# Products of queries and keys as four column tiles, and new sequences of steps, in a fused RWKV-7 and gated-FFN layer

## The chip, the cores and the metric

One NeuronCore of a Trainium2 chip. The metric is the device time of one call in microseconds. All tensors are float32.

## The reference

The input is normalised over its 256 channels; a recurrent attention block (RWKV-7 with 4 heads of 64) and a gated FFN both read the normalised input, and their product is added to the input. Cut to what matters:

```python
# x: (2, 4096, 256)
xn = layernorm(x)
# attention: token-shift mixes, projections to r, w, k, v, kk, a, g, then per head
S = S * d_t + (S a_t) b_t^T + v_t k_t^T       # a_t = -kk, b_t = kk * a, d_t = exp(w_t)
y_t = S r_t
s = (groupnorm(y) * ln_w + ln_b + (r.k.faaaa).v) * g @ w_output.T
# FFN with integer weights / 127
f = silu((silu(xn @ wg.T) * (xn @ wu.T)) @ wd.T)
out = x + s * f
```

The recurrence is computed in chunks of 32 steps. Within a chunk each step's query reads the keys of the earlier steps (for `a`) or of the earlier steps and its own (for `r`), so a matrix of 32 keys by 32 steps is wanted for each of two kinds of query (`a`, `r`), two kinds of key (`k`, `b`), each head and each batch; a mask keeps the part below the diagonal.

## The kernel before

**Tiling.** The 4096 steps are cut into 16 blocks of 256 steps of both batches (512 columns, 8 chunks of 32 steps for each batch; `NT` = 16, `L` = 32). Channels lie on the partitions in two halves (`NH` = 2, two heads each).

**Sections.** The outer loop runs over sections. In section i, block i+1 is normalised and mixed (`norm`, letter L), block i goes through projections and keys (`mixing` F, `decays` D, `key` K, `receptance` R, `value` V, `update` E, `pairs` X), block i-1 through the FFN (`ffn` N) and the recurrence (`back` B), block i-2 through the output (`output` O). On each engine every stage is a generator that yields after each step; the order of the steps is written out by hand as a string of letters for each engine (`ORDER`, with `FIRST` and `LAST` for the sections at the ends), and `walk` takes one step of the named stage for each letter. So each engine's instruction order is fixed, and the engines meet only at semaphores.

**PSUM.** Four banks form a ring (`ring`, `room` waits until a bank's last content was taken); four more (`chunk_banks`) belong to the recurrence and, early in a section, to the projections.

**Pairs.** `pairs` goes through a block in four quarters `qt` (one half of the channels, that is two heads on the 128 partitions, by 4 of the 8 chunks, `n`, with the batch `b` inside). VectorE makes the keys of a quarter in `KSb`: for each group `j` of 8 steps, 64 columns, 32 for the keys `k` and 32 for the keys `b`, each scaled for that group (steps `near`, `far`, `keys`). ScalarE makes the queries in `qpad`, 32 columns for each chunk and group: two heads (each with zeros on the other head's partitions) by two kinds of query by 8 steps. On TensorE the steps `half` and `matrix` multiply them (line 509): weights are the 64 keys of one chunk and group, 128 partitions, the 32 columns of queries stream, and the result goes to 64 partitions of the bank, partitions 0 to 63 for batch 0 and 64 to 127 for batch 1. All 64 keys are multiplied for each group `j`, also those that lie behind the group's steps; VectorE's `copy_predicated` (line 1156) takes from the bank only what the mask lets through. The step `KT` transposes the keys for the state (line 517). The ring's bank for quarter `qt` is free again when VectorE's copy is done (`am_ready`).

**Back.** For each of 8 chunks `c` the recurrence goes TensorE (`state`, line 614), ScalarE (`rhs`, line 904), TensorE (`u`, line 628), VectorE and ScalarE (lines 1206, 910), TensorE (`s`, line 642), VectorE (state, line 1211), with GpSimd's fading of the state (line 1325) beside it; the outputs `values` (589) and `y` (598) fill in.

Names used below: `gate..`, `up..`, `down..` are the FFN's products (lines 534 and 544), `k0`, `k1`, `hk`, `gh`, `v..` projections (line 380), `out0`, `out1` the output's products (line 664).

Of the kernel before, what the change touches and what calls it, by code (L numbers as in the profile page):

```python
# [21 lines left out]
L = 32  # L22
BL = 8
# [24 lines left out]
for _n, _w in (("ident", 128), ("bd", 128), ("center", 128), ("am0", 256), ("ti", HL * HL)):  # L48
# [1 line left out]
    _at += _w  # L50
CTOT = _at

ORDER = {"pe": ("NNNFNKOOFNNORVNNNNKKOVKRBNKBNRNNVBBNBBNBNBNBBVNNBBEBVBBNBBVBNBBNBBXBXBBNXBBNBNBBXBBXBXBBNBBLBNBBXXBB"
            "LXXXXLL"),
         "act": ("NFKFFFFFRFVNKKNVOKKKBEBOKRKRDXXBXBVNBVNBBVVNBBBXBVVBBXBBBBNBBXXBLBBLXLBXBBNBBLXX"),
         "dve": ("ONBOOBBBBBDBBBBBBBNBBDBBDDOOKKDXEFKKNDEDEXDKEEBXBXXXNBXBXXXBEXXBEXXBXNBXLBXXXBXXBLXBXNXXXBXXXBXLXLBX"
             "XXBBXXLLLLLLLL"),
         "pool": ("DBBBBBBLBBLBLLLLLLLL")}
FIRST = {"pe": ("NFKFKKNNNNNVNNKVRKRVNRVVNNNNNNNNNNNNNNNNNVEXXXNXXXLXXXXXLXLLN"),
         "act": ("NNKFFFNFNNFFKFKVKKKEVKKRRXXDRVVVVVVXXXNNXNLXXLLXXLX"),  # L60
         "dve": ("DNDDDNFKKEDNKKDXEXDDENKEXXXLEXXXXXXLXXXEXEXXXXXXXXNXXXXXXXXXXXLLXXLLLLLLLNL"),
         "pool": ("DLLLLLLLLLL")}
LAST = {"pe": ("NOOONONNNNNNNNNBBNNNBBBBBNBBBBBNBBBBBNBBBBBNBBBNBBNBBBBBNBBBBBNBBBNBBNNNNN"),
        "act": ("NONNOBBNBBBBBBBBNBBBBBBBBBNBBBBBBBBNN"),
        "dve": ("BOOOBBBBBBBBBBBBBBBBONONNBBBBBBBBBBBNBBBBBNBN"),
        "pool": ("BBBBBBBBB")}
NB = 4

class Signal:
# [51 lines left out]
def program(nc, d):  # L121
    with ExitStack() as ctx:
# [128 lines left out]
        pe, act, dve, pool, sp = nc.tensor, nc.scalar, nc.vector, nc.gpsimd, nc.sync  # L251
# [86 lines left out]
        def sections():  # L338
            for i in range(-1, NT + 2):
                yield tuple(t if 0 <= t < NT else None for t in (i + 1, i, i - 1, i - 2))  # L340

        def run(engine, norm, mixing, decays, key, receptance, value, update, pairs, ffn, back, output, convert):
            for tn, tf, tb, to in sections():
                streams, order = {}, LAST if tn is None and tf is None else FIRST if tb is None and to is None else ORDER
                if tn is not None:
# [13 lines left out]
        def pe_program():  # L359

            def room(key, emptied):

                o, before = ring.take(key, emptied)
                if before:
                    pe.wait_ge(*before)
                return o
# [132 lines left out]
            def pairs(t):  # L499
                for qt in range(NK):  # L500
                    K, Q, E = KSb[qt % 2], qpad[qt % 2], KE[qt % 2]
                    o = room((t, "A", qt), am_ready(t, qt + 1))
                    pe.wait_ge(*q_made(t, qt + 1))
                    pe.wait_ge(*keys_made(t, qt + 1))
                    for n in range(QC // 2):
                        for j in range(NJ):
                            for b in range(B):
                                oc = o[64 * b:64 * b + 64, 128 * n:128 * n + 128].rearrange("p (x e) -> p x e", e=L)
                                q = pe.matmul(oc[:, :, BL * j:BL * j + BL], K[:, 2 * n + b, 64 * j:64 * j + 64],  # L509
                                              Q[:, 2 * n + b, j, :, :, :].rearrange("p a b e -> p (a b) e"), start=True, stop=True)  # L510
                        if n == 1:
                            yield f"half{qt}"
                    q.then_inc(*ring.fill((t, "A", qt)))
                    yield f"matrix{qt}"
                    o = room((t, "KT", qt), kt_ready(t, qt + 1))
                    for n in range(QC // 2):
                        q = pe.transpose(o[:, 128 * n:128 * n + 128], E[:, 2 * n:2 * n + 2, :].rearrange("p q n -> p (q n)"), ident)  # L517
                    q.then_inc(*ring.fill((t, "KT", qt)))
                    yield f"KT{qt}"
# [150 lines left out]
            pe.wait_ge(s_set, NSET)  # L670
            pe.wait_ge(s_clear, NCLEAR)
            run("pe", norm, mixing, decays, key, receptance, value, update, pairs, ffn, back, output, convert)


# [841 lines left out]
```

## Time and profile before

| | us |
|---|---|
| median of 3 runs | 1608.94 (1607.33 to 1612.72) |
| span of the profiled execution | 1603.4 |
| around the span, median less span | 5.5 |
| TensorE matmul busy | 1520.5 (95%) |
| VectorE busy | 1243.6 (78%) |
| ScalarE busy | 1069.5 (67%) |
| GpSimd busy | 354.6 (22%) |

The profile counts an engine as busy from an instruction's start to its end; TensorE's matmuls overlap one another, so their busy time is the time in which at least one runs. PE stands for TensorE's matmuls, PEld for its weight loads, DVE for VectorE, ACT for ScalarE, POOL for GpSimd. "A<-B, C" names the tile written and those read, "128*64" the rows and columns of the array, "128x32" the partitions and columns that stream. The chain that ended last is followed back from the last instruction to whatever released each one.

### The profile page before, as it was taken

The page shows a single profiled execution, that of the slowest core. Times are in us where ns is not written, and L with a number is a line of the kernel's source. Part 1 is how long each engine was busy: PE and PEld are TensorE (multiplying, and loading weights), DVE is VectorE, ACT ScalarE, POOL GpSimd, SP SyncE. Part 2 cuts the span into 40 slices and gives each one's busy share as a digit, 9 for nine tenths or more (in the row PEclk, how much of TensorE's full clock was granted, in tenths as well). Part 3 has the DMA queues.
Part 4 walks back from the last instruction along what each step waited for, and adds up shares of the span by engine and source line. Part 5 has one row for each costly group of instructions (what it writes and reads, how often), then busy time and mean ns, then how long its engine had stood idle before and what let it go on. Part 6 is the DMA issues. An engine that isn't in the chain of part 4 may idle for free.

```text
span 1603.4 us, 48245 instructions
## 1 busy us (share of the span) xinstructions
PE 1520.5 (95%) x20288; PEld 1064.9 (66%) x20288; DVE 1243.6 (78%) x2661; ACT 1069.5 (67%) x1889; POOL 354.6 (22%) x362
## 2 busy tenths in 40 slices
PE   3699999999999999999999999999999999999887
PEld 1366767576676757667676676757667675766765
DVE  2968787787878878887887878778787887888643
ACT  3758586685857758685775858668585775768512
POOL 3121402313040131302213140231304013130201
PEclk9799999999999999999999999999999999999999
DMA  4011110301212021111202111030121202111020
GB/s 149 14 25 29 33 34 16 62 18 32 43 25 47 16 55 25 33 34 24 56 16 39 42 34 34 16 62 19 33 42 25 48 16 55 25 33 34 12 56 28
DMA packets 251430, 57.85 MB, mean 36 GB/s; under 512 B 223696, under 2 KB 250704, under 8 KB 251088
## 3 DMA queue, kind: packets, MB, share of 16 engines
q1 hardware_dynamic: 241936, 41.95, 13.9%
q10 hardware_dynamic: 9280, 12.81, 2.2%
q8 instruction: 162, 2.65, 0.7%
q14 instruction: 52, 0.43, 0.1%
HBM read 36.38 MB, written 18.35 MB: 34 GB/s over the span
## 4 chain that ended last, share of the span: by engine, by line
PE 92%; DVE 3%; ACT 2%; issue 1%; POOL 0%; DMA 0%; SPq 0%; ACTq 0%; DVEq 0%; POOLq 0%
PE bank L534 23%; PE chunk L380 15%; PE bank L544 11%; PE bank L509 8%; PE bank L664 4%; PE chunk L642 3%; PE chunk L614 3%; PE chunk L589 3%; PE chunk L598 2%; PE bank L485 2%; PE bank L380 2%; PE bank L517 2%; PE bank L479 2%; PE chunk L628 2%; DVE VU L981 1%
## 5 line engine op out<-in xcount | busy, mean ns | idle before, releaser
L1325 POOL TENSOR_TENSOR SF<-ST,CT 128x256 f32<-128x256 f32 x128 | 99.7, 779 | 728.8 <-DVE ST L1211 728.8
L534 PE MATMUL bank<-xT,wg 128*128 128x256 f32 x768 | 197.2, 391 | 14.2 <-DVE VU L981 13.5
L534 PE MATMUL bank<-xT,wu 128*128 128x256 f32 x768 | 207.3, 395 | 0.0
L544 PE MATMUL bank<-wd,hT 128*128 128x256 f32 x768 | 176.8, 383 | 1.9 <-DVE hT L1171 1.9
L534 PEld LDWEIGHTS bank<-xT,wg 128*128 128x128 f32 x768 | 136.3, 189 | 57.6 <-DVE VU L981 24.1
L544 PEld LDWEIGHTS bank<-wd,hT 128*128 128x128 f32 x768 | 143.3, 190 | 29.3 <-issue 7.2
L534 PEld LDWEIGHTS bank<-xT,wu 128*128 128x128 f32 x768 | 135.1, 188 | 34.8 <-issue 14.5
L380 PE MATMUL chunk<-KS,W 128*128 128x512 f32 x320 | 149.6, 598 | 0.3 <-ACT gT L719 0.3
L509 PE MATMUL bank<-qpad,KS 128*64 128x32 f32 x4096 | 141.2, 226 | 4.0 <-DVE KE L1143 4.0
L887 ACT ACTIVATE Y<-chunk 32x256 f32<-32x256 f32 x256 | 96.3, 376 | 70.9 <-PE chunk L598 67.0
L509 PEld LDWEIGHTS bank<-qpad,KS 128*64 128x64 f32 x4096 | 130.7, 141 | 14.1 <-issue 9.0
L380 PE MATMUL chunk<-big,W 128*112 128x512 f32 (+1 forms) x256 | 117.9, 593 | 5.1 <-POOL big L1284 2.9
L861 ACT ACTIVATE sg<-bank 128x512 f32<-128x512 f32 x96 | 57.1, 595 | 86.4 <-PE bank L534 84.5
L1171 DVE TENSOR_TENSOR hT<-sg,bank 128x512 f32<-128x512 f32 x96 | 65.7, 684 | 53.0 <-ACT sg L861 35.2
L904 ACT ACTIVATE rhs<-chunk 96x256 f32<-96x256 f32 x128 | 48.5, 379 | 87.3 <-PE chunk L614 86.3
L1206 DVE COPY VU<-chunk 32x256 f32<-32x256 f32 x128 | 53.4, 417 | 63.3 <-PE chunk L628 62.1
L380 PEld LDWEIGHTS chunk<-KS,W 128*128 128x128 f32 x320 | 59.2, 189 | 62.9 <-issue 48.5
L830 ACT ACTIVATE qpad<-big 64x256 f32<-64x256 f32 x256 | 92.2, 407 | 1.9
L1284 POOL TENSOR_TENSOR KS<-VU,xT 128x512 f32<-128x512 f32 x64 | 89.0, 1424 | 0.0
L1284 POOL TENSOR_TENSOR big<-VU,xT 128x512 f32<-128x512 f32 x64 | 74.4, 1198 | 48.4 <-DVE VU L981 48.4
L1211 DVE TENSOR_TENSOR ST<-SF,chunk 128x256 f32<-128x256 f32 x128 | 53.8, 420 | 37.2 <-PE chunk L642 34.4
L380 PEld LDWEIGHTS chunk<-big,W 128*112 128x112 f32 (+1 forms) x256 | 46.5, 182 | 49.7 <-issue 39.4
(156 smaller groups left out, 3231.3 us busy)
## 6 DMA issues: line engine op xcount, KB each, us to landing
smalls<-in_x SPq DMA_DIRECT2D x32, 256.0 KB, 3.1
Y<-in_x SPq DMA_DIRECT2D x32, 256.0 KB, 3.0
out<-fsil ACTq DMA_DIRECT2D x32, 256.0 KB, 2.6
scrA<-AM SPq DMA_DIRECT2D x64, 64.0 KB, 1.9
hat<-scrB SPq DMA_DIRECT2D x32, 128.0 KB, 3.1
hat<-scrF SPq DMA_DIRECT2D x32, 128.0 KB, 3.1
KE<-scrA SPq DMA_DIRECT2D x64, 32.0 KB, 2.2
scrT<-KE SPq DMA_DIRECT2D x16, 128.0 KB, 1.7
```

Source lines behind the costliest of these rows:

```text
L380: m = pe.matmul(o, weights[:, h, :], x[:, h, :], start=(h == 0), stop=(h == NH - 1))
L509: q = pe.matmul(oc[:, :, BL * j:BL * j + BL], K[:, 2 * n + b, 64 * j:64 * j + 64], Q[:, 2 * n + b, j, :, :, :].rearrange("p a b e -> p (a ...
L534: q = pe.matmul(o[:, TT_ * n2:TT_ * n2 + TT_], w[:, h, 128 * (n + n2):128 * (n + n2) + 128], x_now[:, h], start=(h == 0), stop=(h == NH - 1))
L544: q = pe.matmul(o[:, 256 * m:256 * m + 256], hT[:, n, 128 * m:128 * m + 128], wd[:, n, :], start=(n == 0), stop=(n == NF - 1))
L664: q = pe.matmul(o[:, 256 * n2:256 * n2 + 256], yb[:, h, 128 * m:128 * m + 128], wo[:, h, :], start=(h == 0), stop=(h == NH - 1))
L830: i = act.activation(Q[p0:p0 + 64, :, :, hh, x, :], own[p0:p0 + 64, qs], ACT.Copy)
L861: act.activation(sg[:, :], ring.tile(key)[:, :], ACT.Silu).then_inc(*sg_ready.up)
L887: i = act.activation(by_batch, RY[64 * x + 32:64 * x + 64, :, :].rearrange("p b (g n) -> p b g n", g=NH), ACT.Copy)
L1171: i = dve.tensor_tensor(hT[:, n:n + 2, :], sg[:, :].rearrange("p (n c) -> p n c", n=2), ring.tile(key)[:, :].rearrange("p (n c) -> p n c", ...
L1211: dve.tensor_tensor(ST[:, :, :, :].rearrange("p b h n -> p b (h n)"), SF[:, :, :, :].rearrange("p b h n -> p b (h n)"), PS, ALU.add).then_ ...
L1284: pool.tensor_tensor(columns(dst[:, h, :]), columns(w[:, h, :]), x_now_of(par, h), ALU.add).then_inc(*moved.up)
L1325: pool.tensor_tensor(SF[:, :, :, :], ST[:, :, :, :], fade[:, c].unsqueeze(3).to_broadcast([128, B, NH, N]), ALU.mult).then_inc(*faded.up)
```

## The change

In `pairs` on TensorE the product of one chunk and group `j` is cut in two calls, one for each kind of key `x`. Each takes only the keys up to the end of the group, `BL * j + BL` = 8, 16, 24 or 32 columns of weights, and writes as many partitions from partition `64 * b + 32 * x` on. So four column tiles of up to 32 columns are used in turn (batch 0 `k`, batch 0 `b`, batch 1 `k`, batch 1 `b`) where two of 64 were used. The streamed queries are the same 32 columns. The strings of steps are new for all sections and all engines but GpSimd's in `FIRST` and `LAST`.

```diff
-ORDER = {"pe": ("NNNFNKOOFNNORVNNNNKKOVKRBNKBNRNNVBBNBBNBNBNBBVNNBBEBVBBNBBVBNBBNBBXBXBBNXBBNBNBBXBBXBXBBNBBLBNBBXXBB"
-            "LXXXXLL"),
-         "act": ("NFKFFFFFRFVNKKNVOKKKBEBOKRKRDXXBXBVNBVNBBVVNBBBXBVVBBXBBBBNBBXXBLBBLXLBXBBNBBLXX"),
-         "dve": ("ONBOOBBBBBDBBBBBBBNBBDBBDDOOKKDXEFKKNDEDEXDKEEBXBXXXNBXBXXXBEXXBEXXBXNBXLBXXXBXXBLXBXNXXXBXXXBXLXLBX"
-             "XXBBXXLLLLLLLL"),
-         "pool": ("DBBBBBBLBBLBLLLLLLLL")}
+ORDER = {"pe": ("NNNFNKOONFNOKKVONNNNRKRVBKBNNRNNBBNBBNVBNBNBBVNBBEBNVBBVBBNBNBBNBBXBXBBXNBBNBXBBNBBXBXBBNBBLBXXBBNBB"
+                "XLXXXLL"),
+         "act": ("NFKFFFFNFFKKNOVORKKKVBEBKKRRXDXBXBNVNBVBBVVBNBBVVXBBBXBBBXNXBBBBLBBXLLBXBBNBBXLX"),
+         "dve": ("OBNOBBOBBBBDBBBBBDBOBBBNBDODKKEXDKKFDNEXEDDKEEBXBXXXNBXBXXEXEBXBXXXXBXXBLNBXXBXXXBXXBXLNXXXXBXXBXLXB"
+                "LXBXBXLLLLLLLL"),
+         "pool": ("BDBBBBLBLBBBLLLLLLLL")}
...
                     for n in range(QC // 2):
                         for j in range(NJ):
                             for b in range(B):
-                                oc = o[64 * b:64 * b + 64, 128 * n:128 * n + 128].rearrange("p (x e) -> p x e", e=L)
-                                q = pe.matmul(oc[:, :, BL * j:BL * j + BL], K[:, 2 * n + b, 64 * j:64 * j + 64],
-                                              Q[:, 2 * n + b, j, :, :, :].rearrange("p a b e -> p (a b) e"), start=True, stop=True)
+                                for x in range(2):
+                                    p0, keys = 64 * b + L * x, BL * j + BL
+                                    oc = o[p0:p0 + keys, 128 * n:128 * n + 128].rearrange("p (x e) -> p x e", e=L)
+                                    q = pe.matmul(oc[:, :, BL * j:BL * j + BL], K[:, 2 * n + b, 64 * j + L * x:64 * j + L * x + keys],
+                                                  Q[:, 2 * n + b, j, :, :, :].rearrange("p a b e -> p (a b) e"), start=True, stop=True)
                         if n == 1:
                             yield f"half{qt}"
                     q.then_inc(*ring.fill((t, "A", qt)))
```

## Rows read from the trace of the kernel before

**Rows 1.** The page: busy us, share of the span, instructions.

```profile
PE 1520.5 (95%) x20288; PEld 1064.9 (66%) x20288; DVE 1243.6 (78%) x2661; ACT 1069.5 (67%) x1889; POOL 354.6 (22%) x362
```

**Rows 2.** The page: chain that ended last, by engine and by line.

```profile
PE 92%; DVE 3%; ACT 2%; issue 1%; POOL 0%; DMA 0%; SPq 0%; ACTq 0%; DVEq 0%; POOLq 0%
PE bank L534 23%; PE chunk L380 15%; PE bank L544 11%; PE bank L509 8%; PE bank L664 4%; PE chunk L642 3%; PE chunk L614 3%; PE chunk L589 3%; PE chunk L598 2%; PE bank L485 2%; PE bank L380 2%; PE bank L517 2%; PE bank L479 2%; PE chunk L628 2%; DVE VU L981 1%
```

**Rows 3.** Busy time by engine in two sections; columns in the first line.

```profile
core 0: us, PE busy (x) PEld busy (x) DVE busy (x) ACT busy (x) POOL busy (x), PEclk, DMA share, GB/s
759.50:854.70 95.20, 93.81 (x1269) 65.89 (x1269) 77.64 (x167) 66.61 (x118) 22.16 (x23) 1.00 0.17 34
664.40:759.50 95.10, 93.43 (x1267) 65.42 (x1265) 76.89 (x166) 66.66 (x118) 21.39 (x22) 1.00 0.16 34
```

**Rows 4.** Waits of PE from 759.5 to 854.7: us, times, longest.

```profile
PE bank L534 <- DVE VU L981: 1.8, 2, 0.9
PE chunk L420 <- issue: 0.4, 1, 0.4
```

**Rows 5.** Busy time of line 509 alone in that section: PE, then PEld.

```profile
759.50:854.70 95.20, 8.62 (x256) 7.95 (x256) 1.00 0.17 34
```

**Rows 6.** The chain in order of time: start us, us, what.

```profile
823.42 1.06 PE bank L509 x32
...
844.14 1.99 PE bank L509 x64
846.12 0.39 PE chunk L642 x16
846.52 0.39 PE chunk L598 x16
846.91 1.91 PE bank L380 x4
```

**Rows 7.** Timeline of PE: start us, us to the last end, instructions merged.

```profile
844.07 2.06 PE L509 MATMUL bank<-qpad,KS 128*64 128x32 f32 x64
846.05 0.46 PE L642 MATMUL chunk<-VU,KT 64*64 64x64 f32 x16
```

**Rows 8.** The chain, at a section's start: streams of 512, 256 and 128 columns.

```profile
762.40 1.72 PE chunk L380 x4
764.11 0.86 PE bank L534 x4
...
766.69 0.87 PE bank L655 x8
```

**Rows 9.** Timeline of PE: weights 64 wide, 64 and 16 columns.

```profile
790.61 1.15 PE L563 MATMUL bank<-hat 64*64 64x64 f32 x32
...
793.70 1.06 PE L571 MATMUL bank<-KE,hat 64*64 64x16 f32 x32
```

**Rows 10.** Timeline of PE: first and last start of two groups of eight.

```profile
843.62 0.28 PE L598 MATMUL chunk<-VU,AM 32*64 32x64 f32 x4
...
843.78 0.22 PE L628 MATMUL chunk<-rhs,TT 32*64 32x64 f32 x1
...
843.81 0.22 PE L598 MATMUL chunk<-VU,AM 32*64 32x64 f32 x1
843.84 0.22 PE L628 MATMUL chunk<-rhs,TT 32*64 32x64 f32 x1
...
843.87 0.22 PE L598 MATMUL chunk<-VU,AM 32*64 32x64 f32 x1
```

**Rows 11.** Section 0: its window (columns of rows 3), then the chain.

```profile
70.70:90.00 19.30, 16.30 (x277) 15.29 (x278) 18.67 (x52) 8.21 (x19) 0.00 (x0) 0.61 0.01 2
...
73.70 3.63 PE bank L509 x64
...
78.37 3.56 PE bank L509 x64
...
84.69 2.56 PE bank L509 x64
...
87.84 1.99 PE bank L509 x64
```

**Rows 12.** Busy time by engine in two stretches (columns of rows 3).

```profile
790.00:795.00 5.00, 5.00 (x79) 3.32 (x78) 4.97 (x9) 4.92 (x8) 0.00 (x0) 1.00 0.24 29
823.00:851.00 28.00, 28.00 (x654) 22.86 (x652) 22.20 (x58) 18.01 (x43) 6.03 (x9) 1.00 0.01 3
```

## What the change will do to the time

> **What bounds the kernel now.** I read the page's busy times and the chain that ended last first. TensorE is busy for 95% of the span, VectorE for 78% [rows 1], and TensorE's matmuls carry 92% of the chain; line 509, the products that the change rewrites, carries 8% of it [rows 2]. Then I cut the span into sections, the outer steps of the kernel. Sections 1 to 15 repeat every 95.1 us at the full TensorE clock, with TensorE busy for 93.4 to 93.8 us and VectorE for some 77 us of each [rows 3]. In one section TensorE waits for another engine twice, for 1.8 us together, both times at the section's start where VectorE works off the mix products [rows 4]. So a microsecond taken from TensorE's stream shortens a section by nearly a microsecond, until VectorE's order of steps becomes the tighter one.
>
> **What line 509 costs now.** A section has 256 of its matmuls [rows 5], two for each call since the operands are f32 (4 quarters x 4 chunks x 4 groups of steps x 2 batches = 128 calls). The chain gives them stretches of 32 in 1.06 us and of 64 in 1.99 us [rows 6]. A stretch of 64 runs from 844.07 for 2.06 us, and one matmul is recorded with 0.22 us, so the last starts 1.84 us after the first: 1.84/63 = 29.2 ns from one start to the next [rows 7]. The remaining 0.12 us of a stretch is its change of array shape; it stays. The two column tiles (batch 0 in columns 0 to 63, batch 1 in 64 to 127) take turns, so one tile is used every 58.4 ns; I call that a slot. A section has 256/2 = 128 slots, 7.5 us.
>
> **What a slot consists of.** A stream of N columns takes 430 ns for 512 (1.72 us for four), 215 ns for 256 and 109 ns for 128 [rows 8], 0.84 ns per column; 32 columns would be 27 ns. The slot of 58 ns is therefore not set by the stream. Line 571 (16 columns) starts every (1.06-0.21)/31 = 27 ns and line 563 (64 columns) every (1.15-0.22)/31 = 30 ns, each on two tiles with weights 64 wide [rows 9]: a fourfold stream makes a tenth of difference. What these rows share with line 509 is the width of the weights, 64. Either the load of 64 columns of weights sets the slot, or a fixed time between two uses of a tile does. No row has weights 32 wide, so the bounds are half of the slot (29 ns, at which the stream of 27 ns would take over) and the whole of it (58 ns). The Trainium skill, "TensorE: Matmul & The Clock Gate", section "LDWEIGHTS (loading the stationary operand)", makes a load proportional to the columns of the weights, P/1.2 ns: 53 ns for 64 and 27 ns for 32. By that price alone the slot would be 27 ns.
>
> **The change, part 1: the products.** It removes the 256 matmuls of 64 weight columns and adds 512 of 8, 16, 24 or 32 columns (mean 20), four column tiles in turn, with the same 32 streamed columns. The stream no longer shrinks with the keys, so a slot is at least 27 ns for each. If all four tiles work side by side, a section has 512/4 = 128 slots, as many as now, and each lasts 29 to 58 ns. That tiles do run side by side is shown where lines 598 and 628 meet: eight starts within 0.03 us, then the next eight 0.06 us later [rows 10], on four row groups with two column tiles each. That is 7.3 ns per matmul; the new stretches want 30/4 = 7.5 ns. That column tiles take part in it is shown by line 642: 16 matmuls of 64 columns (54 ns of stream each) start (0.46-0.22)/15 = 16 ns apart on two row halves and two column halves [rows 7], where the row halves alone would allow 27 ns. What no row shows is four column tiles over all 128 rows. I take a slot of 30 ns, nearest to the weight-width reading with the stream just under it. Saving per section: 128 x (58.4 - 30) = 3.6 us, for sections 1 to 15 54 us. Section 0 runs its products partly at the 1.2 GHz clock (0.61 granted from 70.7 to 90 us): two stretches at 3.56 to 3.63 us, one at 2.56, one at 1.99, 11.7 us in all [rows 11]; by the same share (48%) it saves 5.6 us. Gross: 60 us, with 0 as the other bound.
> The weights' bytes, the queries, the copy under the mask (line 1156) and all transfers stay as they are; products above the mask's steps are no longer written, and the copy doesn't take them. These cost nothing.
>
> **Part 2: the sequences.** They move steps and add none, so the busy times stay. On TensorE `k1`, `hk` and `out1` go ahead of `up02`, `gh` goes behind `gate05`, `up04` behind the inverse's corner products, `half1` ahead of `y4`, `half2` and `matrix2` ahead of `y6`, `KT2` ahead of `mixin`. On VectorE the outputs `out0`/`out1`, `e3`, `mkz`, `k`, `dm` and the two `bonus` steps come earlier, and with them `near1` and `far1`, the keys that `half1` waits for. ScalarE takes `gh` and `v1` later, `KT0` and `q2` ahead of `state5`. GpSimd takes `state0` ahead of the zeroing and the norm's `root` and `x0` ahead of `state5` and `state6`: GpSimd is busy 22 of 95 us [rows 3], and what queues behind `root` (the fading of the state) is due only when the next state product is done. SyncE's queue keeps its order; its waits for `mk1`, `g1` and `out1` are released by steps that move by a few microseconds, and `out1` moves ahead. All of it is covered by TensorE's own work as long as no wait on another engine comes late. Bounds: the section's idle time of TensorE is 95.2 - 93.8 = 1.4 us [rows 3]; taking all of it away gives 21 us, and as much may be lost.
>
> **What is late next.** From 823 to 851 us lies all of a section's line 509; TensorE is busy for 28.0 of these 28 us and VectorE for 22.2 [rows 12]. With 3.6 us less, VectorE would have 22.2 of 24.4 us, 91%, and it takes part in each turn of the recurrence between TensorE's steps (`u`, then `s`). A wait of TensorE for it will show now and then. From 790 to 795 us VectorE is busy 4.97 of 5 us and TensorE 5.00 [rows 12], so a full VectorE need not stop TensorE. I price the return at 0.6 us per section, 10 us in all; its bounds are 0 and the gross gain.
> Sum against the profiled execution: 1603.4 - 60 + 10 = 1553.4 us of span. The median of the runs, 1608.9, lies 5.5 us above that span; with them around the new span as well: **1559 us**.
>
> **Rivals.**
> (a) The slot is a fixed time. For it: lines 571 and 563 have nearly the same slot at 16 and 64 columns [rows 9], and no narrower weights stand in the trace. Against: the slot doubles at half the clock, 3.56/64 = 56 ns per start [rows 11], as work in the array would, though that holds for a fixed number of cycles too. Then 128 slots of 58.4 ns cost what they cost now, and only the sequences act: 1609 us, 1600 to 1618. Chance 0.14.
> (b) Slower: four column tiles over all rows don't start independently, and only two overlap, as now, because the four tiles stream over the same 128 rows, which lines 598 and 628 never do [rows 10]. Then the price of a start is the slot halved, not quartered, 15 ns or more for 512 matmuls. The point from which it decides is 7.5 us / 512 = 14.6 ns per start; at 16 ns a section grows by 0.7 us, 11 us in all, 1620 us; without any overlap (30 ns) by 7.9 us, some 125 us, 1735 us. Chance 0.09.
> (c) Slower by a floor of starts in the long run. The shortest run of starts with rows, 32 of lines 598 and 628 from 843.62, follows long matmuls, behind which instructions can collect; over 844.07 to 846.91 (line 509, then 642 and 598) 96 matmuls take 2.84 us, 30 ns each [rows 6, 7]. If a sustained floor lay at 25 ns, the 512 would take 12.8 us, 5.3 us more per section and 85 us in all: 1694 us. The eight starts in 0.03 us speak against a floor of single starts [rows 10]; a sustained one isn't excluded by rows. Chance 0.07. By this rule (the Trainium skill, "TensorE: Matmul & The Clock Gate", "Wait — 56ns, not 53.3ns?") starts never come closer than some 25 ns however short the stream; the trace has 7 ns across tiles and so bears it out at most for one tile.
>
> **How the numbers follow.** Forecast 0.70: gross 60, return 10. Its own range is 1542 (nothing returned, part of the idle time gone) to 1592 (slot of 38 ns or more waits). The range of 8 in 10 takes in (a) and the mild form of (b): 1542 to 1620. What a measurement of this kernel can tell from no change is about 0.3%, 4.8 us. Faster: 0.70 and a third of (a), less a few in a hundred for sequences that miss, 0.71. Within 0.3%: most of (a), 0.12. Slower: (b), (c) and the sequences, 0.17.
>
> **What the profile after would show.** Line 509 with 8192 matmuls of 128 rows by 32 columns or fewer, and stretches of 128 in some 1.1 us and of 64 in 0.6 us; starts 7 to 8 ns apart. TensorE's busy time down by some 55 us, a section of 92 us, VectorE at 80% or more, and a few new waits of TensorE for it in the second half of a section. Stretches of 128 in 2 us mean (a), in 2.1 to 4 us (b) or (c); stretches as short as forecast with a section still over 94 us mean that VectorE or the new sequences took the gain, and then the waits list must name who.

## The result and the profile after

The changed kernel takes 1647.5 us (median of 4 runs, 1634.8 to 1657.7), the kernel before in the same rounds 1610.8 us (1607.3 to 1612.9). The ratio is 1.0232, with a 95% interval of 1.0184 to 1.0279: slower by 2.3%, where a time lower by 3% was forecast. The four executions differ with the clock, from 1634.8 us at a mean granted clock of 0.983 to 1657.7 us at 0.963. The profiled execution, of 1650.6 us, has a span of 1649.1 us.

The page of after (busy times, the granted clock in 40 slices, the queue of TensorE's instructions, the chain that ended last by engine) answers to [rows 1] and [rows 2]. The second fence is the instruction queue's line on the page of before.

```profile
PE 1520.8 (92%) x24384; PEld 1031.4 (63%) x24384; DVE 1275.5 (77%) x2661; ACT 1089.5 (66%) x1904; POOL 343.7 (21%) x362
PEclk9799999999999999999999999999999999999967
q8 instruction: 194, 3.18, 0.8%
PE 71%; DVE 11%; issue 8%; POOL 5%; ACT 3%; DMA 1%; SPq 0%; ACTq 0%; DVEq 0%; POOLq 0%
```

```profile
q8 instruction: 162, 2.65, 0.7%
```

TensorE is busy for as long as before, but in a longer span: its share of the chain fell from 92 to 71%, and 8% of it is now "issue", time in which TensorE waited for nothing that the profile shows. TensorE has 4096 more matmuls and as many more weight loads, 8192 instructions, and the instruction queue carries 32 more packets and 0.53 MB more: 256 instructions of 64 bytes in each packet of 16 KB.

A section now takes 95.2 to 101.4 us and 97.7 us in the mean of 13 (95.24 before), counted from its first transposition of keys (`KT`) to the next section's. One of them and line 511 alone (line 509 before), with the columns of [rows 3] and [rows 5]:

```profile
646.80:744.10 97.30, 93.11 (x1533) 63.35 (x1525) 79.59 (x166) 68.01 (x120) 21.28 (x22) 0.98 0.17 34
...
646.80:744.10 97.30, 6.01 (x513) 5.03 (x513) 0.98 0.17 34
```

The products did get shorter, 8.62 to 6.01 us. What is beside them did not hold. The waits of PE over the whole run (us, times, longest), to be read against [rows 4], which is of one section:

```profile
PE bank L511 <- issue: 16.1, 18, 1.8
...
PE bank L536 <- DVE VU L983: 13.4, 15, 1.0
PE bank L666 <- DVE hat L1240: 11.8, 15, 3.0
PE chunk L630 <- issue: 8.6, 8, 1.8
...
PE chunk L600 <- issue: 5.5, 3, 2.2
```

All waits for "issue" together are 38.5 us, in before 6.5. The timeline of PE and the chain show one from close by, answering to [rows 6] and [rows 7]:

```profile
646.81 0.74 PE L511 MATMUL bank<-qpad,KS 128*8 128x32 f32 x64
647.48 0.46 PE L616 MATMUL chunk<-ST,hat 64*64 64x64 f32 x16
647.87 0.52 PE L511 MATMUL bank<-qpad,KS 128*8 128x32 f32 x40
650.22 0.38 PE L511 MATMUL bank<-qpad,KS 128*16 128x32 f32 x24 [1.83 <-issue]
```

```profile
646.88 0.67 PE bank L511 x54
647.55 0.39 PE chunk L616 x16
647.94 0.45 PE bank L511 x40
648.39 1.83 issue
650.22 0.38 PE bank L511 x23
```

The stretch of 64 is what was forecast: one matmul is recorded with some 0.2 us, so 0.54/63 = 8.6 ns from start to start, a slot of 34 ns on each of four tiles. Then TensorE stands still for 1.83 us in the middle of a loop that waits for no engine.

The account of the spans, from the busy times of the whole run (line 509, 510 or 511 alone; all other matmuls; the rest of the span), the waits for "issue", and the time at the lower granted clock (0.50, the 1.2 GHz level) added up from the clock records. The last three rows are the mean of the 13 sections from the first `KT` of section 1 to that of section 14; they leave out the start and the end of the run. Each column is one execution.

| us | before | e1: products | e2: sequences | e7: e2, yT1 back | after | e9: after, yT1 back | e8: short weights, yT1 back |
|---|---|---|---|---|---|---|---|
| products' line | 141.2 | 93.5 | 139.1 | 139.1 | 94.0 | 93.0 | 118.5 |
| other matmuls | 1379.3 | 1411.1 | 1390.7 | 1392.8 | 1426.8 | 1397.6 | 1382.2 |
| no matmul | 82.9 | 130.5 | 91.7 | 83.3 | 128.3 | 121.5 | 82.5 |
| span | 1603.4 | 1635.2 | 1621.4 | 1615.2 | 1649.1 | 1612.1 | 1583.2 |
| waits for issue | 6.5 | 45.5 | 4.4 | 6.6 | 38.5 | 40.8 | 5.5 |
| at clock 0.50 | 37.8 | 71.5 | 47.0 | 71.5 | 105.8 | 60.6 | 38.4 |
| of it after 1500 us | 14.0 | 23.7 | 23.1 | 47.6 | 47.8 | 26.5 | 21.3 |
| a section | 95.24 | 97.05 | 96.35 | 95.30 | 97.72 | 96.34 | 94.05 |
| other matmuls in it | 85.20 | 86.79 | 85.56 | 85.06 | 86.96 | 86.08 | 85.13 |
| no matmul in it | 1.43 | 4.45 | 2.17 | 1.62 | 4.94 | 4.46 | 1.58 |

### The profile page after: what moved, and what is told of

Its sections match the earlier page's. It is cut to its first block, busy times and chain, and to the rows that moved or that the text cites. A ratio compares the mean times of both kernels' runs of the same rounds, so it can differ in the third digit from the quotient of the medians.

```text
span 1649.1 us, 56452 instructions
## 1 busy us (share of the span) xinstructions
PE 1520.8 (92%) x24384; PEld 1031.4 (63%) x24384; DVE 1275.5 (77%) x2661; ACT 1089.5 (66%) x1904; POOL 343.7 (21%) x362
## 4 chain that ended last, share of the span: by engine, by line
PE 71%; DVE 11%; issue 8%; POOL 5%; ACT 3%; DMA 1%; SPq 0%; ACTq 0%; DVEq 0%; POOLq 0%
PE bank L536 17%; PE chunk L380 12%; PE bank L546 11%; PE bank L511 4%; PE chunk L644 3%; POOL big L1286 3%; PE chunk L591 3%; PE chunk L616 3%; PE chunk L600 3%; POOL st L1333 2%; PE bank L479 2%; PE bank L666 2%; PE bank L485 2%; PE chunk L630 2%; DVE hat L1235 2%
## 5 line engine op out<-in xcount | busy, mean ns | idle before, releaser
L1327 POOL TENSOR_TENSOR SF<-ST,CT 128x256 f32<-128x256 f32 x128 | 88.9, 695 | 671.6 <-DVE ST L1213 671.6
L536 PE MATMUL bank<-xT,wg 128*128 128x256 f32 x768 | 207.4, 400 | 13.4 <-DVE VU L983 13.4
L546 PE MATMUL bank<-wd,hT 128*128 128x256 f32 x768 | 186.9, 398 | 3.0 <-DVE hT L1173 1.7
L546 PEld LDWEIGHTS bank<-wd,hT 128*128 128x128 f32 x768 | 149.6, 198 | 34.4 <-issue 9.0
L536 PEld LDWEIGHTS bank<-xT,wu 128*128 128x128 f32 x768 | 140.0, 194 | 33.1 <-issue 7.8
L380 PE MATMUL chunk<-big,W 128*112 128x512 f32 (+1 forms) x256 | 123.6, 618 | 6.6 <-ACT gT L721 3.4
L511 PE MATMUL bank<-qpad,KS 128*8 128x32 f32 (+3 forms) x8192 | 94.0, 199 | 23.8 <-issue 16.1
L511 PEld LDWEIGHTS bank<-qpad,KS 128*8 128x8 f32 (+3 forms) x8192 | 81.1, 101 | 44.9 <-issue 40.5
L1145 DVE TENSOR_TENSOR KS<-KB,EF 128x128 f32<-128x128 f32 (+1 forms) x256 | 87.9, 395 | 0.5
```

The lines of the kernel that those rows point to most:

```text
L380: m = pe.matmul(o, weights[:, h, :], x[:, h, :], start=(h == 0), stop=(h == NH - 1))
L536: q = pe.matmul(o[:, TT_ * n2:TT_ * n2 + TT_], w[:, h, 128 * (n + n2):128 * (n + n2) + 128], x_now[:, h], start=(h == 0), stop=(h == NH - 1))
L546: q = pe.matmul(o[:, 256 * m:256 * m + 256], hT[:, n, 128 * m:128 * m + 128], wd[:, n, :], start=(n == 0), stop=(n == NF - 1))
L1145: i = dve.tensor_tensor(o, z[:, qs, 0:i4, :], fac, ALU.mult)
L1327: pool.tensor_tensor(SF[:, :, :, :], ST[:, :, :, :], fade[:, c].unsqueeze(3).to_broadcast([128, B, NH, N]), ALU.mult).then_inc(*faded.up)
```

## The experiments

The theories. **F**, supply: TensorE's instructions arrive in packets of 256 and not faster than one in some 3 to 4 us; line 511 with a start every 8.6 ns, a weight load beside each, uses up a packet in 128 starts, 1.1 us. **C**, clock: the lower clock comes by itself with the short products and stops included cost little. **W**: the width of the weights sets the slot; against it the forecast's rivals (a), a fixed slot, and (b), only two column tiles overlapping. For the sequences **Y**: one wait, for the step `yT1`, costs the time; **V**: VectorE's key steps run beside GpSimd's fading and slow each other.

**e1_products and e2_sequences.** Each half of the change alone: the new products with the old strings, and the old products with the new strings.

```diff
-ORDER = {"pe": ("NNNFNKOONFNOKKVONNNNRKRVBKBNNRNNBBNBBNVBNBNBBVNBBEBNVBBVBBNBNBBNBBXBXBBXNBBNBXBBNBBXBXBBNBBLBXXBBNBB"
-                "XLXXXLL"),
+ORDER = {"pe": ("NNNFNKOOFNNORVNNNNKKOVKRBNKBNRNNVBBNBBNBNBNBBVNNBBEBVBBNBBVBNBBNBBXBXBBNXBBNBNBBXBBXBXBBNBBLBNBBXXBB"
+            "LXXXXLL"),
...
```

The diff is that of e1 against after, and goes on in the same way for every engine and for `FIRST` and `LAST`; e2 is before with the other strings, the mirror image.

> The new products with the old sequences of steps on every engine. The profile of the changed kernel has the products as short as forecast (64 starts in 0.54 us, 8.5 ns apart), but TensorE stands still 29 times for 0.5 to 2.4 us inside or right behind such stretches, and always at the same place of its instruction stream: when the instruction whose number leaves 193 on division by 256 is due. A packet of instructions is 16 KB, that is 256 instructions of 64 bytes. Theory F (fetch): TensorE takes its instructions in packets of 256, and the next packet comes no sooner than some 3.3 us after the last; the new products put two instructions in 8.5 ns. Then the old sequences have the same trouble, since they put the products into the same crowd of short matmuls: the old chain with the products shortened is 1549 us, packets held to 3.0 to 3.3 us add 46 to 60 us, spells at half clock behind the longest stops some 10 to 20, so 1605 to 1635 us with over 25 stops. Theory S (sequences): the new sequences are what is slow; then with the old ones the forecast comes true, 1555 to 1570 us. Theory C (clock): half-clock spells come from the narrow products themselves and not from the stops: then spells stand here without a stop ahead of them.

> The old products (64 columns of weights, two tiles) with the new sequences. Theory F: no packet is used up in less than 3.3 us, so no stops over 0.5 us and no half-clock spells in the middle; only what the order of the steps does remains, 1600 to 1625 us (the new VectorE order shows a wait of 0.8 us per section ahead of line 666, 11.8 us against 5.5, and the last sections after the last products are 99 us long against 86). Theory S: 1650 to 1690 us, since the products' 55 us of gain are missing and the sequences stay bad.

Measured: e1 1639.5 us (1636.7 to 1640.8), ratio 1.0190 (1.0169 to 1.0212); e2 1625.9 us (1622.8 to 1631.1), ratio 1.0119 (1.0092 to 1.0146). Both halves are slower than before, the products by 30 us and the sequences by 16; together they cost 37, less than the sum. e1 lies 4 us above the range that F had given it. Its waits for issue are longer than after's:

```profile
PE bank L511 <- issue: 23.1, 17, 1.9
```

e2 has one such stop, of 0.57 us, and the clock is at 1.00 throughout its middle: the many stops and the lower clock there belong to the products. Its own loss has two candidates, the wait of line 664 and the key steps. Waits of PE in e2, then VectorE's line 1143 (ns min/median/max) in e2 and in before:

```profile
PE bank L664 <- DVE hat L1238: 12.0, 15, 3.0
```

```profile
L1143 DVE TENSOR_TENSOR KS<-KB,EF x256: 282/347/731, 72.2 to 1524.4; 128x128 f32<-128x128 f32 x64, 128x192 f32<-128x192 f32 x64
```

```profile
L1143 DVE TENSOR_TENSOR KS<-KB,EF x256: 280/319/398, 71.9 to 1511.8; 128x128 f32<-128x128 f32 x64, 128x192 f32<-128x192 f32 x64
```

**e3_one_kind.** After with one kind of key only: half of its products, two column tiles of up to 32.

```diff
-                                for x in range(2):
+                                for x in range(1):
...
+    mask[key == 1, :] = 0
```

> The changed kernel with the products of the key kind k alone; those of the kind b are left out and masked away, so half of the 512 matmuls of a section are gone, as many are left as before the change, and they use two column tiles of up to 32 columns. Theory F: the same array time per section if a tile's slot of 34 ns sets it (256 x 17 ns = 4.4 us, as 512 x 8.5), but half the instructions; no stops over 0.5 us, no half-clock spells in the middle, 1560 to 1590 us. If the pace is one start per 8.5 ns whatever the tiles, the stretches of 32 take 0.27 us instead of 0.54. Theory S: the sequences are the same, so the time stays over 1630 us. Theory C: spells stay.

Measured: 1582.0 us (2 runs, 1579.0 and 1585.0), ratio 0.9835 (0.9801 to 0.9870), within what F had given it. The kernel leaves out half of the products, so its time says nothing of a usable version. The instruction count is that of before, and the waits for issue fall from 38.5 to 7.4 us, with no lower clock in the middle. Three stops, of 0.77 to 1.39 us, are left, where none over 0.5 us was expected. Timeline of PE:

```profile
734.15 1.13 PE L511 MATMUL bank<-qpad,KS 128*8 128x32 f32 x64
```

(1.13 - 0.2)/63 = 14.8 ns per start on two tiles, a slot of 29.5 ns. By the width of the weights, 8, 16, 24 and 32 columns, a group of four starts takes 59, 58, 58 and 63 ns in the median, slots of 29.5, 29, 29 and 31.5 ns: up to 24 columns the width makes no difference. Narrow weights do pay; after's loss is in what its second half adds. With the sequences of e2 in both, e3 lies 43.9 us below it.

**e4_short.** Before with nothing changed but the width: both kinds of key stay in one matmul, which takes only as many keys `b` as the mask lets through (40, 48, 56 or 64 columns). No instruction is added.

```diff
-                                oc = o[64 * b:64 * b + 64, 128 * n:128 * n + 128].rearrange("p (x e) -> p x e", e=L)
-                                q = pe.matmul(oc[:, :, BL * j:BL * j + BL], K[:, 2 * n + b, 64 * j:64 * j + 64],
+                                keys = L + BL * j + BL
+                                oc = o[64 * b:64 * b + keys, 128 * n:128 * n + 128].rearrange("p (x e) -> p x e", e=L)
+                                q = pe.matmul(oc[:, :, BL * j:BL * j + BL], K[:, 2 * n + b, 64 * j:64 * j + keys],
```

> The kernel before with its old sequences and two column tiles, but weights of 32 + 8, 16, 24 or 32 columns in place of 64: the keys of the kind b behind the group's steps are left away, those of the kind k stay, so no matmul is added. Theory W (the slot is the load of the weights, 0.84 ns per column and 5 ns): slots of 39, 45, 52 and 58 ns, a stretch of 32 matmuls in 0.82 us instead of 0.93, 1.3 us per section, 1585 to 1593 us. If the slot is fixed for every weight wider than 32: 1604 to 1613 us. Theory F: no packet of 256 instructions is used up faster than 3.3 us but for one or two, so no stops over 0.5 us and no half-clock spell in the middle.

Measured: 1591.6 us (1590.5 to 1595.7), ratio 0.9892 (0.9831 to 0.9952), as W had it. Timeline of PE, where before has 2.06 us [rows 7]:

```profile
748.09 1.74 PE L510 MATMUL bank<-qpad,KS 128*40 128x32 f32 x64
```

A group of four starts with weights 40, 48, 56 and 64 wide takes 77, 90, 103 and 117 ns in the median, slots of 38.5, 45, 51.5 and 58.5 ns: 0.83 ns for each column and 5 ns. By the Trainium skill, "TensorE: Matmul & The Clock Gate", section "LDWEIGHTS (loading the stationary operand)", a load takes P/1.2 ns for P columns; the trace agrees in the slope, and has some 5 ns on top. Two stops of the recurrence, of 0.88 and 0.64 us, stand where before has its two of 0.56 us; W holds, and F's "no stops over 0.5 us" was a little too strict.

**e5_mixed.** e4 with the narrow products of after in two of the eight groups of a section (the first halves of quarters 2 and 3), so that few instructions are added in one place.

```diff
+                                narrow = 2 * qt + n // 2 in (4, 6)
+                                for x in range(2 if narrow else 1):
+                                    p0, keys = 64 * b + L * x, BL * j + BL + (0 if narrow else L)
```

> As e4_short, but two of the eight stretches of a section (the first halves of quarters 2 and 3) use four narrow tiles. Theory F: 25% more matmuls of this line, packets at 3.3 us hold TensorE up for 4 to 7 us over the whole span, no long stops, 1583 to 1593 us: nothing more to be had than with e4_short. Without a limit on instructions: 1582 us or less, 6 us under e4_short.

Measured: 1592.3 us (1590.5 to 1596.2), ratio 0.9900 (0.9828 to 0.9971): nothing over e4. One packet is late, by a stop of 1.03 us at 841.5 us, and the waits for issue are 6.8 us in all (e4 7.3), so late packets are not what kept the gain away. The narrow groups themselves gave little. Timeline of PE, a stretch of 64 narrow and 32 short matmuls:

```profile
838.29 1.66 PE L512 MATMUL bank<-qpad,KS 128*8 128x32 f32 x96
```

e4's stretch of 64 takes 1.74 us, and the products' line 115.5 us over the whole run against e4's 118.3. Why each mixed stretch saves only 0.08 us isn't shown, and e5 decides nothing between F and its rival.

**e6_shift.** e1 with 32 products at the very start of TensorE's program, 128 instructions, half a packet. It adds this little work.

```diff
+            for _ in range(32):
+                pe.matmul(bank[0][0:32, 0:32], con[:, 0:32], con[:, 0:32], start=True, stop=True)
```

> e1_products with 32 more small products (128 instructions, half a packet) on TensorE at the very start, where it waits for the first block anyway. Theory F: the stops stay at instructions whose number leaves 193 on division by 256, counted with the new ones, so they come half a packet earlier in the program and fall into other stretches; their number (31) and the time (1635 to 1645 us) change little. If the stops belonged to places in the program (a bank, a semaphore, a transfer), they would move on by 128 instructions, to a rest of 65.

I numbered TensorE's records (matmuls, weight loads, semaphore instructions) by start and took the stops of 0.45 us and more that end with a step of the recurrence or of the products, with the last packet of the instruction queue that started before TensorE went on. Four of the stops of after, and two of e6:

```
kernel  record  mod 256  went on at us  stop us  packet started  took us
after    10177      193         373.99     2.45          371.09     1.43
after    15297      193         551.40     1.84          548.69     1.25
after    18369      193         650.22     2.02          647.60     1.34
after    31937      193        1055.83     2.08         1053.12     1.29
e6        3009      193         162.42     1.62          159.71     1.23
e6       10433      193         375.40     1.73          373.02     1.13
```

(The stop is from start to start, and so a little longer than in the waits.) Between 100 and 1500 us after, e1 and e6 have 27 such stops each at a record of remainder 193 (30, 32 and 30 with those that end at another step), and TensorE goes on 2.1 to 2.9 us after the start of a packet. Before has two, of 0.56 us each, at the same remainder. Gaps of 0.45 to 0.57 us stand at other remainders too, 30 in before and e1, 31 in e6 and 50 in after; all of them are behind a matmul whose stream alone takes 0.43 us (512 columns, or 256 at the lower clock), and I don't count them as stops. A stop that belonged to a step of the program, its banks or its semaphores would have moved by the 128 instructions put ahead, to remainder 65; it stays with the number of the instruction. So TensorE waits for its own instructions. The packets say the same from their side: between 100 and 1500 us no two of them start less than 3.2 us apart in any of the twelve traces, in before they start 6.8 us apart in the median and in after 5.8. The two executions took 1630.0 us (mean granted clock 0.977) and 1654.6 us (0.958); e1's four took 1636.7 to 1640.8 us at 0.976 to 0.979. One execution at e1's clock can't tell whether the time changed.

**e7_yt1.** e2 with one letter moved: VectorE's `yT1` (lines 1233 and 1238) ahead of the recurrence's steps `inv0` and `inv1` again, as in before.

```diff
-         "dve": ("OBNOBBOBBBBDBBBBBDBOBBBNBDODKKEXDKKFDNEXEDDKEEBXBXXXNBXBXXEXEBXBXXXXBXXBLNBXXBXXXBXXBXLNXXXXBXXBXLXB"
+         "dve": ("OBNOOBBBBBBDBBBBBDBOBBBNBDODKKEXDKKFDNEXEDDKEEBXBXXXNBXBXXEXEBXBXXXXBXXBLNBXXBXXXBXXBXLNXXXXBXXBXLXB"
```

> e2_sequences with one step of VectorE put back: yT1 of the output ahead of inv0 and inv1, as in the old sequence. In e2_sequences TensorE waits 12.0 us for line 1238 ahead of line 664, 15 times, against 5.5 us in 2 waits before. Theory Y: this wait is part of the 16 us that the new sequences cost, then it goes back to some 5.5 us and the time to 1617 to 1621 us. Theory V: what costs is VectorE's work itself, 31 us more busy time because its key steps (line 1143) now run against GpSimd's fading of the state, 105 steps overlap it (15 and 90 of two shapes) against 30 before; then the wait goes but the time stays within 4 us of 1626.

Measured: 1607.7 us (1603.1 to 1616.8, 10 runs), ratio 0.9988 (0.9951 to 1.0024). The wait goes:

```profile
PE bank L664 <- DVE hat L1238: 3.0, 1, 3.0
```

VectorE is still busy for 1269.5 us (e2 1274.9, before 1243.6), so the overlap of V is there; TensorE waits 4.1 us longer for line 1143 (8.1 us against 4.0 in before), and the time of the kernel doesn't show it. (The overlap is larger than expected: beside line 1325 run 120 steps of line 1143 in e2 and in e7, 90 of them of the shape 128x128, and 45 in before, none of that shape.) Y holds as the cause. The expectation read the waits wrongly, though. The 5.5 us of before are two waits at the end of the run; the 12.0 us of e2 are 14 of 0.64 us, one in each section, and one of 3.0 us at the end, the one that e7 keeps. So 9.0 us of waits went, and with them more: a section of e2 lasts 96.35 us and one of e7 95.30, 1.05 us less, of which 0.55 is time without a matmul and 0.50 is busy time of the other matmuls. Fifteen times 1.05 us are 15.8 of the 18 us.

**e8_short_yt1.** The short weights of e4 with the sequences of e7.

> The short weights of e4_short with the new sequences, yT1 put back as in e7_yt1. If the two act apart, 1607.7 less 18 (what e4_short gained on the kernel before) = 1590 us, the same as e4_short within 5 us; if the new sequences use the freed time of TensorE better, as they were made for shorter products, under 1585 us.

Measured: 1585.9 us (1583.3 to 1590.9), ratio 0.9863 (0.9841 to 0.9884): 1.4% faster than before and, by the two ratios, 3.6% faster than after. That is within 5 us of the 1590 us that was expected if the two changes act apart. Of the versions that leave nothing out it has the lowest time, but its interval overlaps with that of e4 (0.9831 to 0.9952).

```profile
PE 1500.7 (95%) x20288; PEld 1036.7 (65%) x20288; DVE 1269.5 (80%) x2661; ACT 1087.8 (69%) x1904; POOL 344.2 (22%) x362
```

**e9_after_yt1.** After with the same letter moved.

> The changed kernel (four narrow tiles, new sequences) with yT1 alone put back. Theory F with the sequences' loss apart: 1647 less 18 = 1629 us, still over 1620 since the stops of TensorE for instructions stay (25 or more at a rest of 193). If the lost time were all the sequences', under 1590 us.

Measured: 1614.6 us (1608.1 to 1627.0, 10 runs), ratio 1.0051 (1.0021 to 1.0080). It gained 33 us where 18 were expected, and lies under the 1620 us that F had as its bound. The stops are all still there, 27 between 100 and 1500 us, with the waits for issue at 40.8 us:

```profile
PE bank L511 <- issue: 17.4, 20, 1.6
```

What shrank is the time of the other matmuls, by 29 us, and with it the time at the lower clock, from 105.8 to 60.6 us, of which at most half (23 us) is time lost. From after to e9 the profiled span fell by 37.0 us. Of these, 20.5 lie in sections 1 to 14 (1.38 us each in 13 of them, against 1.05 from e2 to e7), 10.5 in the end of the run from the last section's products on, and 5.9 in its start. At the end after has 47.8 us at the lower clock and e9 26.5; but e7, without a late packet and with the time of before, has 47.6 there, so this part comes and goes between executions and is no gain of the letter. Why five spells at the lower clock stand in the middle of e9 and eight in after's, I can't say from these runs.

**e10_dense.** Before, with 1024 calls on four column tiles, weights 32 wide and 32 streamed columns, waiting for nothing, behind its last output: what F says about supply, measured by itself.

```diff
+            pe.wait_ge(*stored(NT - 1))
+            for i in range(1024):
+                p0 = 32 * (i % 4)
+                pe.matmul(bank[0][p0:p0 + 32, 0:32], con[:, 0:32], con[:, 32:64], start=True, stop=True)
```

> The kernel before, and after its last output is stored 4096 more matmuls (1024 calls) of 32 columns of weights and 32 streamed columns on four column tiles in turn, with nothing to wait for: 8192 instructions, 32 packets. Theory F: the first 100 or so start 7 to 9 ns apart, then each 128 matmuls (256 instructions) take 2.3 to 3.5 us whatever the tiles could do, 75 to 110 us in all. Without a limit on instructions: 1.0 to 1.1 us for each 128, 35 us in all; at half clock twice that, 70 us, but then evenly spaced and without gaps.

These 1024 calls are 2048 matmuls, 4096 instructions and 16 packets; the expectation doubled each of them. The span is 1658.4 us, 55 more than before. Timeline of PE, then two windows with the columns of [rows 3]:

```profile
1607.15 1.55 PE L676 MATMUL bank<-con 128*32 128x32 f32 x128 [2.13 <-issue]
1610.89 1.93 PE L676 MATMUL bank<-con 128*32 128x32 f32 x128 [2.20 <-issue]
1614.64 1.93 PE L676 MATMUL bank<-con 128*32 128x32 f32 x128 [1.81 <-issue]
1618.11 1.94 PE L676 MATMUL bank<-con 128*32 128x32 f32 x128 [1.54 <-issue]
```

```profile
1604.00:1614.00 10.00, 4.50 (x379) 4.12 (x365) 0.00 (x0) 0.00 (x0) 0.00 (x0) 0.69 0.02 5
1614.00:1624.00 10.00, 5.80 (x384) 5.39 (x384) 0.00 (x0) 0.00 (x0) 0.00 (x0) 0.50 0.02 5
```

The first 219 matmuls start without a stop, 8.5 ns apart. From then on TensorE gets 128 matmuls with their loads, 256 instructions, and stops, again at remainder 193. From one group to the next it is 3.47 to 3.75 us; the last group starts at 1657.66 us, and 50.5 us for 14 groups from 1607.15 on is 3.61 us each, 14.1 ns per instruction and 28 ns per matmul. That is just above the 2.3 to 3.5 us that was expected. Nothing but the instructions can be late there: one loop, no waits, all operands in place. F is shown.

## Why the prediction was wrong

**The slot (right, one term a little off).** The slot is 34 ns, forecast 30 with bounds of 29 and 58. e4's slope of 0.83 ns per column shows that the width of the weights sets it from 40 to 64 columns; e3's 29 ns at 8, 16 and 24 columns lies next to the stream's 27, which was forecast to take over. What makes it 34 and not 30 on four tiles isn't shown. Four column tiles over all 128 rows run side by side: 8.6 ns per start. Rivals (a) and (b) are refuted. The products' line went from 141.2 to 94.0 us, 47 us less, against 60 forecast: (58.4 - 34.3) x 128 is 3.1 us per section and not 3.6.

**The instructions (the step that failed).** I counted 512 matmuls for 256 and priced the starts, the weights' bytes and the transfers, but the instructions themselves at nothing. What hid them in before is the long matmuls around: two packets came late there, by stops of 0.56 us in the recurrence (at 730.9 and 1397.6 us); I had not seen these two, and they were the warning. In after the recurrence and the products, both of short matmuls, lie so close together that 30 packets come late between 100 and 1500 us, and the waits for issue are 38 us in all. I had rival (c), a floor of 25 ns on sustained starts, and gave it 0.07. Its number was nearly that of e10 (28 ns), and its remark that instructions collect behind long matmuls was the mechanism; but it charged all 512 matmuls, 85 us, where only some packets are late. The 96 matmuls in 2.84 us that it named [rows 6, 7], 30 ns each, were the densest long run it had, while the change wanted 128 in 1.1 us; a run that dense had no row, and I went on as if the eight starts in 0.03 us [rows 10] covered it. By the Trainium skill, "TensorE: Matmul & The Clock Gate", section "Wait — 56ns, not 53.3ns?", starts are never closer than some 25 ns; the traces differ for single starts (7 to 9 ns across tiles) and come near it in the long run, for another reason, the packets.

**The clock (not in the prediction).** Before has no stretch at 0.50 between 100 and 1500 us, after has eight, of 3.4 or 6.8 us. The windows of a stop and of what follows it, columns of [rows 3]:

```profile
371.60:374.00 2.40, 0.16 (x4) 0.08 (x4) 0.97 (x3) 0.70 (x2) 0.00 (x0) 1.00 0.00 0
374.30:377.60 3.30, 3.30 (x33) 2.64 (x18) 2.76 (x7) 1.13 (x3) 0.00 (x0) 0.50 0.03 5
```

Through the stop TensorE is busy for 0.16 us of 2.4 and the clock is granted in full; then it is at 1.2 GHz for 3.4 us. Each of the eight begins 0.2 to 1.7 us after the end of one of the twelve longest stops (1.58 to 2.45 us from start to start); four of the twelve have none behind them. e1, e6 and e9 have four, six and five such stretches in their middle, each with a stop of 1.4 us or more just ahead, and in one of e1's the clock fell 0.35 us before TensorE went on. C as a cause of its own falls: e2, e3, e4, e5, e7 and e8, which have at most three stops, none over 1.4 us, have no such stretch. Half of the 68 us more at the lower clock, 34 us, lies in these eight, and at half speed costs up to 17 us. The other half lies after 1500 us (47.8 us against 14.0); the first 100 us have 23.9 in both. That half can't be laid to the stops: e7 has 47.6 us there without a late packet. In the sections the account closes. The other matmuls take 1.76 us more in each of them (86.96 against 85.20), of which at most 1.05 is the lower clock, some 0.46 are the tails of the last matmuls ahead of the stops (0.22 us each), and 0.36 is what e2 has as well and e7 has not.

**The sequences (the second step that failed).** "All of it is covered by TensorE's own work as long as no wait on another engine comes late": one came late in each of 14 sections, by 0.64 us. `yT1` went behind `inv0` and `inv1` on VectorE, and `out0` on TensorE needs it. I had listed what moved earlier on VectorE and not asked of each step that moved later who waits for it. I had bounded the sequences with 21 us either way, and 16 were lost. e7 takes them back with one letter: 1.05 us in each section, 0.55 of time without a matmul and 0.50 of matmuls' time. How a wait lengthens the matmuls around it by as much isn't shown. The new strings for `FIRST` and `LAST` cost nothing that shows: e7 keeps them and has the time of before.

**The return of 10 us on VectorE.** VectorE was not what came next. In e8, with the products 23 us shorter, it is busy for 80% and TensorE is without a matmul for 82.5 us, as before. That was priced at the wrong engine, and with no loss in it.

**The sum.** Forecast -60 + 10. Measured from span to span: -47 for the products' line, +45 without a matmul (32 more of it for issue, about 6 for line 666), +47.5 for the other matmuls, together +46. Of these 46 us some 33 lie in sections 1 to 14 (2.48 us in each of 13) and 12 after the start of the last section's products, mostly in the lower clock there that e7 has too; by the medians the kernel is slower by 37 us. My check named beforehand, "stretches as short as forecast with a section still over 94 us", is what came (0.74 us and 97.7 us); I had put VectorE or the sequences behind it. By e2 and e7 the sequences are 1.05 to 1.1 us of a section, and the late packets, with the clock behind them, are the rest: 2.4 us of waits for issue in each section, which alone nearly use up the 2.8 us that the products give.

## What to carry to other kernels

Splitting a small matmul across column tiles pays only where the extra instructions find cover: count instructions (a load and a matmul each, twice for f32) against the packets of 256, and look for the densest 256 in the trace; under some 3.5 us for 256, as these traces have it, they will be late wherever no long matmuls stand ahead. Shortening the weights without adding instructions (e4) gave 1.1% where splitting them cost 1.9%. When an order is changed, ask of every step that moves later who waits for it on another engine; a single letter was worth 18 us here.

## What the hardware did that I had not expected

- TensorE's instructions come in packets of 256; with nothing else to wait for it gets one in 3.47 to 3.75 us (e10), 28 ns per matmul with its load, and in no trace do two packets between 100 and 1500 us start less than 3.2 us apart. Late packets show as "issue" at one fixed remainder of the instruction's number.
- After eight of the twelve longest stops of after the granted clock went to 1.2 GHz for 3.4 or 6.8 us, after TensorE had gone on, so that such a stop may cost up to another 1.7 or 3.4 us. In e1 it was three of the twelve longest.
- VectorE's line 1143 (two inputs in SBUF, 128x128) takes 286 ns in the median alone (38 in e2), and 506 ns in the mean and up to 731 ns beside GpSimd's line 1325 (90 in e2). Timeline of VectorE and GpSimd in e2:

```profile
827.43 1.47 DVE L1143 TENSOR_TENSOR KS<-KB,EF 128x128 f32<-128x128 f32 x4
...
827.59 0.62 POOL L1325 TENSOR_TENSOR SF<-ST,CT 128x256 f32<-128x256 f32 x1 [4.58 <-DVE ST L1211]
```

Four of them take 1.47 us there, 368 ns each. By the Trainium skill, "SBUF — State Buffer", section "SBUF: two separate sides", such a pair of instructions excludes one another on a shared pair of ports; the trace agrees in kind. Line 1143 is busy for 160.5 us in e7 and 141.4 us in before, 19 us more of VectorE's busy time (26 us more in all), and the kernel's time is the same within 0.5%.
